# Storing the transposed second-layernorm rows as two fp16 halves, and loading them in the shared blocks instead of transposing there

## The reference

```python
x = x + xattn(layernorm(x), ctx, ctx, mask, Wq, bq, ..., Wo, bo, 16)
xf = layernorm(x).reshape(-1, 256)
a, g = split(xf @ Ws1 + bs1); ys = (a * gelu(g)) @ Ws2 + bs2         # shared
logits = (xf @ Wr + br) / 1.5                                        # router, 12 experts
top_val, top_idx = top_k(logits, 2); w = softmax(top_val)
yr = sum over the two picked experts e of w_e * geglu(xf @ We1[e] + be1[e]) @ We2[e] + be2[e]
x = x + ys + yr
```

## Time and profile before

| | us |
|---|---|
| median of 3 runs | 1044.87 |
| lowest, highest | 1041.36, 1046.91 |
| the profiled execution | 1048.87 |
| its span, first to last instruction | 1047.10 |

### The profile page before, as it was taken

How to read it: one execution, slowest core, us unless ns; L and a number is a source line. 1 busy time by engine, 2 the same in 40 slices (tenths; PEclk the granted TensorE clock), 3 DMA queues, 4 the chain that set the end, 5 groups by cost and what they waited for, 6 DMA issues and landing times.

```text
span 1047.1 us, 26810 instructions
## 1 busy us (share of the span) xinstructions
PE 940.2 (90%) x7515; PEld 689.8 (66%) x7515; DVE 714.2 (68%) x1842; ACT 568.1 (54%) x1276; POOL 376.9 (36%) x537
## 2 busy tenths in 40 slices
PE   6578899999998887979999799999799999999996
PEld 4223444545454345858878689888688888898885
DVE  5776778887787735647686666777457677667753
ACT  2126565565555466324544666667346666667653
POOL 5310212445445263142420343445223543434342
PEclk9879999999999999989999999999999999999998
DMA  4552324263552042147654553555225534535232
GB/s 147 141 107 71 104 72 107 79 183 104 125 152 85 22 159 67 62 142 258 214 183 125 163 137 48 144 134 143 36 37 133 135 65 129 135 50 144 44 54 42
DMA packets 107928, 117.34 MB, mean 112 GB/s; under 512 B 20397, under 2 KB 99961, under 8 KB 107649
## 3 DMA queue, kind: packets, MB, share of 16 engines
q1 hardware_dynamic: 87168, 67.97, 23.8%
q0 software_dynamic: 20064, 47.20, 18.1%
q10 hardware_dynamic: 560, 0.53, 0.1%
HBM read 73.91 MB, written 38.87 MB: 108 GB/s over the span
## 4 chain that ended last, share of the span: by engine, by line
PE 42%; issue 5%; DVE 3%; DMA 3%; ACT 1%; DVEq 1%; SPq 0%; ACTq 0%; another core or an unknown queue 0%; POOL 0%; POOLq 0%
PE ff_psH L2312 25%; PE ff_psY L2339 13%; PE ff_psX L2266 2%; PE ff_psH L2281 2%; DVE ff_actf L2565 1%; DMA ff_xrow<-expert_in 1%; PE ff_psY L2296 1%; DMA expert_in<-ff_zeros 1%; DVE ff_actl L2558 1%; ACT ff_gel L2406 1%; DMA out_dram<-ff_x 0%; DVE ff_ysb L2641 0%; DMA ff_x<-out_dram 0%; ACT ff_acth L2401 0%
## 5 line engine op out<-in xcount | busy, mean ns | idle before, releaser
L2312 PE MATMUL ff_psH<-xh,ff_wx 128*128 128x256 f16 (+1 forms) x1776 | 269.5, 263 | 16.2 <-issue 10.6
L2312 PE MATMUL ff_psH<-xl,ff_wx 128*128 128x256 f16 (+1 forms) x888 | 217.4, 263 | 0.0
L1126 DVE TENSOR_REDUCE fast_negm<-fast_psS 128x2 f32<-128x512 f32 x256 | 168.4, 686 | 70.2 <-PE fast_psS L514 68.2
L886 ACT ACTIVATE fast_PT<-fast_psT 128x512 f32<-128x512 f32 x256 | 147.3, 596 | 107.1 <-PE fast_psT L546 104.4
L2247 POOL DMA_INDIRECT out_dram<-ff_ysc,ff_trow x78 | 124.6, 1598 | 193.5 <-ACT ff_ysc L2454 179.2
L2312 PEld LDWEIGHTS ff_psH<-xh,ff_wx 128*128 128x128 f16 x1776 | 166.7, 99 | 38.2 <-issue 15.1
L2565 DVE SCALAR_TENSOR_TENSOR ff_actf<-ff_psH,ff_b1T,ff_gel 128x256 f32<-128x256 f32 (+1 forms) x234 | 106.0, 454 | 101.2 <-ACT ff_gel L2406 99.5
L2406 ACT ACTIVATE ff_gel<-ff_psH,ff_b1T 128x256 f32<-128x256 f32 (+1 forms) x234 | 105.4, 451 | 82.2 <-PE ff_psH L2312 62.9
L2339 PE MATMUL ff_psY<-ff_wx,ff_acth 128*128 128x256 f16 x792 | 132.5, 273 | 0.8 <-DVE ff_actl L2558 0.5
L514 PE MATMUL fast_psS<-fast_Kz,fast_Qs 128*128 128x512 f16 x256 | 100.8, 398 | 33.3 <-DVE fast_negm L1126 23.5
L2401 ACT ACTIVATE ff_acth<-ff_actf 128x256 f16<-128x256 f32 (+1 forms) x282 | 110.6, 392 | 35.6 <-DVE ff_actf L2565 34.1
(11 more groups left out here) (276 smaller groups left out, 1681.5 us busy)
## 6 DMA issues: line engine op xcount, KB each, us to landing
ff_st<-in_L_ffn_We_dram POOLq DMA_DIRECT2D x12, 1536.0 KB
ff_xrow<-expert_in SPq DMA_DIRECT2D x41, 256.0 KB
ff_st<-in_L_ffn_We_dram POOLq DMA_DIRECT2D x12, 768.0 KB
fast_Qs<-qstk SPq DMA_DIRECT2D x48, 128.0 KB
fast_xbuf<-in_x_dram SPq DMA_DIRECT2D x8, 512.0 KB, 5.3
fast_words<-in_mask_BxSxS_bk_dram SPq DMA_DIRECT2D x8, 512.0 KB
fast_xres<-in_x_dram SPq DMA_DIRECT2D x8, 512.0 KB, 4.2
out_dram<-fast_x1s SPq DMA_DIRECT2D x8, 512.0 KB, 5.2
```

Source lines behind the costliest of these rows:

```text
L886: nc.scalar.activation(PT[:, n % NPT, :], psT[n % 2][:], ACT.Exp).then_inc(sem["exp_done"], 1)
L1126: nc.vector.tensor_reduce(negm[:, two(b), t, 2 * p:2 * p + 2], src, AX.X, ALU.max, negate=True).then_inc(sem["max_done"], 1)
L2312: mm = nc.tensor.matmul(psH[j % stage.banks][:, (half + 1) * NB - rows:(half + 1) * NB], a[:, dt, lo:lo + P], x[:, dt, NB - rows:], start= ...
```

## The change

Attention now makes the fp16 halves once a batch. ACT casts `x2T`, which it has just filled, to a new tile `x2h` (`x2_high`, two instructions of 128x512), POOL subtracts it from `x2T` into `x2l` (`x2_low`, two of 128x512), and SP stores both, 256 KB each, in a DRAM tensor `rows_T` (`save_x2`). Each shared block loads its part, 256 KB, into one of two tiles `x16` (`load_x` in the tail, `load_shared` in `feed_forward`), and PE reads the halves from there. `rows_T`, the shared blocks' `row_transposes`, `row_high` and `row_low` are gone, and the copy from `xn2` to `xrow` too. The experts' blocks are as they were. Space is made by letting `odd_keys` work in place; its next load waits for that.

```diff
@@ sync, attention
+        def save_x2(b):
+            until_sp("x2_low", of("x2_low", b, DT))
+            for part, tile in enumerate((x2h, x2l)):
+                sp.dma_start(scratch["x2"][bass.ds(b, 1), :, part * DT:(part + 1) * DT].rearrange("o p t q -> p (o t) q"),
+                             tile[:]).then_inc(sem["x2_saved"], 16)
...
             if b == B - 1:
+                early_blocks.load_x(sp, 0)
+                early_blocks.load_x(sp, 1)
                 until_sp("st_mm", of("st_mm", B - 2, 0))
...
             if real(b + 3):
                 load_ctx(b + 3, 0)
+            if real(b - 2):
+                save_x2(b - 2)
...
         early_blocks.load_rows(sp, 1)
+        early_blocks.load_x(sp, 2)
         early_blocks.store_rows(sp, 0)
         early_blocks.load_rows(sp, 2)
         save_x1(B - 1)
+        early_blocks.load_x(sp, 3)
+        save_x2(B - 1)
         early_blocks.store_rows(sp, 1)
         early_blocks.load_rows(sp, 3)
+        early_blocks.load_x(sp, 4)
         early_blocks.store_rows(sp, 2)
+        early_blocks.load_x(sp, 5)
@@ tensor, tail (five such lines)
-            early_blocks.rows_T(pe, 0)
@@ scalar, attention
         def set_x2T(b, dt):
             until(act, "r_mm", of("r_mm", b, 0))
+            until(act, "x2_low", of("x2_low", b, 0))
...
+        def x2_high(b, dt):
+            until(act, "x2_set", of("x2_set", b, dt + 1))
+            until(act, "x2_saved", of("x2_saved", b, 0))
+            nc.scalar.activation(x2h[:, dt, :], x2T[:, dt, :], ACT.Copy).then_inc(sem["x2_high"], 1)
...
-            exp(b, 2, 3, 4, 5, 6, 7, 8, 9)
+            exp(b, 2, 3, 4, 5, 6)
+            if real(b - 2):
+                x2_high(b - 2, 0)
+            exp(b, 7, 8)
+            if real(b - 2):
+                x2_high(b - 2, 1)
+            exp(b, 9)
...
-            early_blocks.row_high(act, 2)
             set_x2T(last, 0)
             set_x2T(last, 1)
-            gates(2)
-            early_blocks.row_high(act, 3)
+            gates(2, lambda: x2_high(last, 0), lambda: x2_high(last, 1))
@@ vector, tail (five such lines)
-            early_blocks.row_low(dve, 0)
@@ gpsimd, attention
+        def x2_low(b):
+            until(pool, "x2_high", of("x2_high", b, DT))
+            for dt in range(DT):
+                nc.gpsimd.tensor_tensor(x2l[:, dt, :], x2T[:, dt, :], x2h[:, dt, :], ALU.subtract).then_inc(sem["x2_low"], 1)
...
             if real(b - 1):
                 res_bias(b - 1)
+            if real(b - 2):
+                x2_low(b - 2)
             rows_of_two(2, 11)
@@ feed_forward
-        def load_shared(m, u):
-            until(shared, "xT_mm", of(shared, "xT_mm", m - 1))
-            sp.dma_start(xrow[:, u], keep["xn2"][:, bass.ds((m + EARLY) * NBT, NBT), 0:D])\
+        def load_shared(two, u):
+            until(shared, "h_mm", of(shared, "h_mm", two * 2 + u - 1))
+            rows = scratch["x2"][bass.ds(two + EARLY // 2, 1), :, :, u * NB:(u + 1) * NB]
+            sp.dma_start(x16[u][:].rearrange("p s t n -> p (s t) n"), rows.rearrange("o p s n -> p (o s) n"))\
```

More of the change, by code:

```diff
@@ L1737, in _ @@
     def _(sp):
-        blocks.load_rows(sp, 0)
-        blocks.load_rows(sp, 1)
+        for m in range(2):
+            blocks.load_x(sp, m)
+            blocks.load_rows(sp, m)
         for m in range(EARLY):
+            blocks.load_x(sp, m + 2)
             blocks.store_rows(sp, m)
@@ L1769, in _ @@
         for m in range(EARLY):
-            blocks.row_low(dve, m)
             for j in range(SH_PAIRS):
@@ L1776, in _ @@
             blocks.result(dve, m)
-        blocks.row_low(dve, EARLY)
     ctx.close()
@@ L2303, in over_few, with ffn @@
             of_pair(EX_PAIRS - 1, False, True)
-        def ffn(stage, m, wa, wb, more, rows=NB, between=None):
+        def ffn(stage, m, wa, wb, x, more, rows=NB, between=None):
             n = stage.pairs
+            xh, xl = (x[:, part] for part in range(2))
             def hidden(j, half, terms, begins, ends):
@@ L2323, in ffn @@
                     hidden(j, 0, of_low, False, True)
-                for half in range(0 if j else 1, 2):
+                for half in range(1 if j == 0 and halves_come else 0, 2):
                     mm = hidden(j, half, [of_high[0], of_low[0], of_high[1]], True, True)
@@ L2346, in shared_block @@
         def shared_block(m, u, more=None, between=None):
[L2347 removed]
+            shared.until(pe, "odd_loaded" if u else "even_loaded", (m - (2 + u)) * 8 + 16)
+            ffn(shared, m, s1, s2, x16[u], more, between=between)
         for m in range(2):
[L2350 removed]
+            pe.wait_ge(early[f"x_in{m}"], 16 * (EARLY // 2 + 1))
+            ffn(shared, m, s1, s2, x16[m], None)
         pe.wait_ge(b_loaded, 32)
```

177 lines of the change are left out of this document (80 added, 97 removed).

## The result

The changed kernel took 1064.61 us (median of 4 runs, 1062.18 to 1066.38), the kernel before 1045.47 beside it. The two medians are 19.1 us apart. By either the change made the kernel slower. The forecast was 1047.8, with a range up to 1052.5. The profiled execution took 1065.29 us, its span is 1063.7 (before: 1047.1), so the trace has 16.6 us more to explain.

The account below looks back on a forecast made before the run. PE was taken to have little idle time, PE and DVE to run in step in attention, DVE to bound the list blocks. Removed −5.1 and added +8.0 gave +2.9 on the median 1044.87: 1047.8 us, range 1040.5 to 1052.5.

Parts of the forecast that it names:

- item 11: DMAs: new stores and loads of halves cost 0; without cover in the tail, 2 to 5 us would show once.
- Items 7 and 8: Attention: POOL's subtractions delay DVE's layernorm in slots 2 to 4, +4.5, and small operations in slots 5 and 6, +1.5.
- Item 9: ACT's casts (x2_high): free in slots 2 to 6, +1.0 in slot 7 where exponentials run back to back.
- Item 5: List blocks of feed_forward: DVE is the bound, so removing row_low gains 3 times 0.65, −1.95.
- Item 1: Begin of early block 0: PE's transposes and wait for xl go, 1.6; two casts ahead of the gelu; −1.5 taken.
- Item 2: Before the last router: ACT's cast of the block's rows, ahead of copies PE waits for, goes; −0.45.
- Item 10: End of early block 2: casts and a POOL subtraction delay low halves; picks and PE's ranks move by +1.0.
- Item 4: Shared blocks: blocks 0 to 2 gain 0.7 from row_low and 0.5 from loads and transposes; blocks 3 to 6 gain 0.
- Item 6: Last two shared blocks: the first expert's rows come late, so PE's 0.44 each is waiting time anyway; 0.
- the third: Rival: PE is the bound, so everything taken from it counts; −8.5, 1036.4 us, chance 0.10.
- the second: Rival: POOL's subtractions meet nothing that matters; −3.6, 1041.3 us, chance 0.25.
- The fourth: Rival: more collisions, and casts delay exponentials in slots 2 to 6 as well; +7.4, 1052.3 us, chance 0.20.

Follow-up runs that it names:

- run 13: Changed kernel with early loads behind the shared weights' loads and stores behind the next slot's maxima, subtractions left in place: 1062.42 us, ratio 1.0120 to the kernel before.
- run 5: Changed kernel with early loads behind the weights, stores behind the next maxima, POOL's subtractions at slot end behind odd_keys: 1057.83 us, ratio 1.0078 to the kernel before.
- run 3: Changed kernel with stores behind the next slot's maxima and POOL's subtractions at the end of its slot, without a wait: 1067.67 us, ratio 1.0196 to the kernel before.
- run 1: Changed kernel with the two early loads of halves behind the shared weights' loads in slot 7: 1059.63 us, ratio 1.0106 to the kernel before.
- run 7: Run 1 without casts or subtractions; zeros stored once and loaded by every shared block: 1057.15 us, ratio 1.0047 to the kernel before.
- run 8: Run 5 with DVE's first list operation behind the gate of pair 0 instead of pair 1: 1056.35 us, ratio 1.0063 to the kernel before.
- run 11: Run 8 with PE's code shifted by 16 products, the last two casts behind the last high half, their store last: 1051.05 us, ratio 1.0021 to the kernel before.
- run 9: Changed kernel with 16 unused one-column products in a never-taken branch, shifting PE's later code: 1061.87 us, ratio 1.0137 to the kernel before.
- run 10: Changed kernel with 6 unused one-column products in a never-taken branch, shifting PE's later code: 1063.72 us, ratio 1.0164 to the kernel before.
- run 4: Changed kernel with POOL's first expert weight loads held until PE finished the first shared block's hidden products: 1067.85 us, ratio 1.0202 to the kernel before.

## Why the prediction was wrong

The sign of the sum was right, its size was not: +2.9 forecast, 16.6 in the trace. Of the 13.7 us between them slot 7 has 4.8, the shared blocks of `feed_forward` 3.6, the tail 2.5, slots 2 to 6 1.2, and the ends of the trace 1.6, which is scatter. The steps that failed are item 11, which put the new transfers at nothing, and a term that is missing, PE's stop in block 0. By the steps:

- **Items 7 and 8 (collisions), +6.0, right in mechanism and sum.** PE's waits for the maxima grew by 5.5 us; by runs 13 and 5 the collisions cost 4.4 in the time and 5.6 to 8.0 in the traces. Two of four instructions were held, `fast_xn` took 2.85 against 2.9 forecast in slot 2, and 2.49 and 2.54 in slots 3 and 4. PE's wait grew by 1.49, 0.87 and 1.07, 3.4 in all against 4.5. A subtraction takes 1.16 us, not 1.4. The working was looser than its result: two instructions at 1.4 and two at 0.34 are 3.5 us, not 3.1. In slot 5 it was not the picks that were held (0.31 us, as before) but two operations ahead of them; that the sum fits there is in part luck. The Trainium skill's rule of exclusion for a whole instruction gave the right size here (SBUF — State Buffer, Who interferes with whom): the trace agrees, the two held instructions of slot 2 take 1.05 and 1.24 us and end 0.14 and 0.16 behind a subtraction. The instruction of run 3 was held longer, for two subtractions, which stays unexplained.
- **Item 11 (DMAs), 0, failed.** Its reason for the stores was "nothing waits but the next slot's maxima some 8 us later"; they came 1.8 us later, the round trip of slot 3 grew by 1.2, and PE waited 1.4 for it in slots 3 and 4. For the early loads it named no neighbour in the queue at all, and they went ahead of the shared weights, for which ACT, and so PE, was already waiting 1.11. The transfer of 2 to 5 us that "would show once" was named for the tail; it showed in slot 7 instead: 4.4 in ACT's wait, and 5.4 in the slot with PE's half clock behind it (2 to 5.5 over all traces, run 1). The waiting already there was in the trace of before.
- **Item 9 (casts in slot 7), +1.0, about right, somewhat high.** With item 11's part away, slot 7 adds 0.4 to 0.8, and 0.2 in run 7, which has no casts.
- **Item 5 (list blocks), −1.95, failed.** "DVE is the bound" was read from a stretch that ends at the first gate. One gate on DVE has 0.66 idle. What sets the block is a loop over PE, ACT and DVE; runs 8 and 11 shortened it by moving what stands in it. The block itself gained nothing: 8.87 against 8.88.
- **Item 1, −1.5, right in its mechanism, and eaten.** From the transposes to the first product of early block 0 it takes 4.18 us in the kernel before, 2.51 where the clock stays up (runs 7, 9 and 13), so the gain is 1.67; in the changed kernel it takes 4.67, with the clock at 0.50 behind PE's wait of 3.16. But a wait of 3.20 left the clock at 1.00 in run 13 and in the kernel before, so the wait's length alone doesn't decide.
- **Item 2, −0.45, right**: the stretch fell from 14.95 to 14.46. **Item 10, +1.0, right**: +1.3 (14.02 to 15.31).
- **Item 4 (blocks 0 to 2 and 3 to 6), −1.2, right in part.** Blocks 1 and 2 together are 0.4 shorter. Blocks 1 to 11 gave 4.1 in all, more than the 3.15 forecast, but mostly in blocks where nothing was forecast, which is luck. Blocks 5 to 7 gave 1.8 more that wasn't forecast, in about half of the runs; in the others they stay at 9.0 to 9.5 us each with DVE waiting for residual rows as in the earlier trace rows. Item 6 put the last two blocks at 0; in this trace the last one is 1.3 shorter (11.55 to 10.23), and no run tells why.
- **Missing: where the code lies.** The sum had no term for the stop in block 0, +4.6 with the lower clock behind it. The change takes 20 transposes out of PE's tail, ahead of this stage. The likely reading is that a piece of PE's code that came unnoticed before now comes at the 12th product. Runs 9 and 10 show that the stop hangs on the position, run 4 that it hangs on the transfers of the weights. In the trace the queues for instructions carry packets at the entry and again in the 10 us behind it, while the DMA engines are 0.77 to 1.0 busy. But the kernel before and run 9, which have no stop, carry such packets 2 to 6 us behind the entry as well, and no row tells whose they are. That PE waits for the fetch of code fits all this; it isn't shown.

The rivals: the third (PE the bound, 1036.4) and the second are refuted. The fourth came nearest in time, but not by its mechanism: ACT's exponentials weren't late for casts (PE's waits for `fast_PT` in slots 2 to 6 are 2.2 us before and 2.5 now).

What stays open: what decides between the two lengths of blocks 5 to 7 (±2 us); why ACT waits for the weights 5.52 us in one execution of the changed kernel and 2.71 in another; why the experts' stage takes 471 us in one kernel with the code shifted by 16 products and 475 to 476 in the two others; and what PE waited for in block 0.

## What to carry to other kernels

Price a new DMA by its neighbours: which small transfer with someone waiting stands behind it in the queue, read from the start times and not from the slot. Work moved to POOL cost nothing here only where DVE reduced from PSUM; where that is can be read from DVE's timeline, and the subtractions moved there gained 4 to 8 us. And where a change shortens the code ahead of a jump into a stage that begins with large transfers, look for a new stop marked "issue"; unused code in a branch never taken tells in one run whether its position is the cause. Read that from the trace of the stage: the stop was gone in run 9, and the time was hardly better.

## What was not expected of the hardware

- A DVE instruction of 0.26 us took 2.71 beside two back-to-back POOL instructions of 1.16 each, while the layernorm's were let in between two such; three reductions from PSUM beside such a pair took their usual 1.89.
- PE stood still for 3.5 and 5.3 us at a point that moved by exactly 6 products when 6 unused ones were put in front, and vanished with 16.
- A round trip of 16 KB through DRAM took 1.4 to 3.3 us in the kernel before. With two stores of 256 KB just ahead it took 3.2 to 5.5 in slots 3 and 4, and 1.4 to 2.7 in slots 5 and 6, where it took 1.4 and 2.3 before.
- Behind waits of 3.2 and 4.6 us PE ran for about 4 us at half clock (8 products in 1.97 us against 1.09). Behind waits of 3.20 us at the same place, in the kernel before and in runs 7, 9 and 13, it did not.
